# Expert layer with capacity: the last expert's share read straight from its result, sums for two token tiles per addition

## The reference, cut to what matters

```
logits = einsum('GSM,ME->GSE', x, router_w)          # 8 groups of 128 tokens, 8 experts
dispatch, combine = _gating_top2(logits, C)          # C = 32 places per expert and group
expert_inputs = einsum('GSEC,GSM->EGCM', dispatch, x)
hidden = gelu(einsum(expert_inputs, w0)) * einsum(expert_inputs, w1)
expert_outputs = einsum('EGCH,EHM->EGCM', hidden, wo)
out = einsum('EGCM,GSEC->GSM', expert_outputs, combine)
x = x + out
x = x + cross_attention(layernorm(x), ctx, ...)      # the next layer
```

## Time and profile before

| | |
|---|---|
| median of three runs | 1238.1 us |
| the profiled execution's own time | 1238.72 us |
| its span | 1237.0 us (1.7 us lie around it) |
| TensorE busy | 1145.1 us, 93% of the span |
| TensorE weight loads | 732.2 us, 59% |
| VectorE busy | 544.9 us, 44% |
| ScalarE busy | 450.2 us, 36% |
| GpSimd busy | 244.2 us, 20% |
| mean granted TensorE clock | 0.963 |

### The profile page before, as it was taken

One profiled execution on the slowest core, in us unless ns is written; L12 is line 12 of the kernel. 1 busy time (PEld: TensorE's weight loads), 2 busy tenths in 40 slices (PEclk: granted clock), 3 DMA queues, 4 the chain that ended last, 5 costly groups with the idle time before them and its releaser, 6 DMA issues. The chain is left out here.

```text
span 1237.0 us, 19157 instructions
## 1 busy us (share of the span) xinstructions
PE 1145.1 (93%) x7215; PEld 732.2 (59%) x7239; DVE 544.9 (44%) x1553; ACT 450.2 (36%) x591; POOL 244.2 (20%) x366
## 2 busy tenths in 40 slices
PE   6989999999859999999779999999987699999996
PEld 4443333333447888888656333333326699999995
DVE  4657777773362111121157776666406322212111
ACT  4556666666422111111143455555652101110110
POOL 4652222225000000000004000000200233333331
PEclk9999999999959999999989999999998799999998
DMA  8646222001172333345349221120004599999971
GB/s 224 166 150 159 42 40 43 3 1 50 53 273 51 136 136 136 136 147 195 65 180 210 38 39 39 40 40 1 1 1 160 202 372 377 314 321 310 318 231 47
DMA packets 87926, 168.53 MB, mean 136 GB/s; under 512 B 9474, under 2 KB 61396, under 8 KB 85252
## 3 DMA queue, kind: packets, MB, share of 16 engines
q1 hardware_dynamic: 80132, 157.99, 40.5%
q0 software_dynamic: 5152, 6.05, 2.5%
q10 hardware_dynamic: 2560, 3.41, 1.0%
HBM read 147.30 MB, written 20.98 MB: 136 GB/s over the span
## 5 line engine op out<-in xcount | busy, mean ns | idle before, releaser
L1213 ACT ACTIVATE prob<-st_ps 128x1024 f32<-128x1024 f32 x256 | 253.8, 1022 | 186.9 <-PE st_ps L1095 105.0
L219 DVE CUSTOM_DVE_ANT_0 junk<-s_ps,bias_rows,mx 128x512 f32<-128x512 f32 x236 | 167.8, 748 | 64.0 <-PE s_ps L204 63.3
L1087 PE MATMUL st_ps<-q_stack,k_stack 100*128 100x512 bf16 x512 | 183.7, 382 | 7.6 <-ACTq L1188 3.5
L219 DVE CUSTOM_DVE_ANT_0 junk<-s_ps,bias_rows 128x512 f32<-128x512 f32 x232 | 153.3, 689 | 66.0 <-PE s_ps L204 65.5
L204 PE MATMUL s_ps<-k_stack,q_stack 97*128 97x512 bf16 x468 | 174.9, 383 | 7.3 <-ACT q_stack L248 5.4
L1600 PE MATMUL h_ps<-expert_in,w 128*128 (+1 forms) x704 | 155.0, 382 | 2.2 <-PEq L66 2.2
L1600 PEld LDWEIGHTS h_ps<-expert_in,w 128*128 128x128 f32 (+1 forms) x704 | 132.7, 189 | 23.0 <-issue 2.4
L1107 PE MATMUL o_ps<-prob,v_unit 128*32 128x512 f32 x1024 | 139.7, 599 | 1.0 <-ACT prob L1213 1.0
L204 PEld LDWEIGHTS s_ps<-k_stack,q_stack 97*128 97x128 bf16 x468 | 44.8, 98 | 140.2 <-DVE mx L219 83.8
L1946 ACT ACTIVATE silu<-gu_ps 128x512 f32<-128x512 f32 x46 | 27.5, 597 | 227.1 <-PE gu_ps L1887 227.1
L1630 ACT ACTIVATE gelu_out<-h_ps 128x256 f32<-128x256 f32 (+1 forms) x88 | 33.7, 383 | 182.2 <-PE h_ps L1600 182.2
(11 more groups left out here) (283 smaller groups left out, 1185.3 us busy)
## 6 DMA issues: line engine op xcount, KB each, us to landing
wg<-in_gateT SPq DMA_DIRECT2D x23, 1024.0 KB
wu<-in_upT SPq DMA_DIRECT2D x23, 1024.0 KB
wd<-in_downT SPq DMA_DIRECT2D x23, 1024.0 KB
w<-in_w SPq DMA_DIRECT2D x16, 1368.0 KB
w<-in_w SPq DMA_DIRECT2D x8, 1280.0 KB
k_scr<-k_parts SPq DMA_DIRECT2D x48, 128.0 KB, 2.3
k_stack<-k_scr SPq DMA_DIRECT2D x16, 384.0 KB, 4.9
k_stack<-k_scr SPq DMA_DIRECT2D x16, 256.0 KB, 5.6
```

The source lines that it names most:

```text
L219: self.pr.nc.vector.tensor_tensor_reduce(out=self.junk[:, self.bank("job", u, j)], in0=self.ps[:, self.bank("job", u, j)], in1=self.m.bias ...
L1087: pe.matmul(st_ps[:, h], stack(K[b], ROWS, i % 2, h, slice(kt * P, (kt + 1) * P)), stack(Q[b], ROWS, i % 2, h, slice(0, SQ)), start=True, ...
L1213: nc.scalar.activation(prob[:, kt % 2, 2 * hp:2 * hp + 2], st_ps[:, 2 * hp:2 * hp + 2], ACT.Exp).then_inc(exp_done, 1)
```

## The change

For the last expert, the columns of `comb` are turned once more, into the layout in which its result already lies: eight products with 32 output rows each, group 4r + q to partitions 32q of half r, in a bank of the router; VectorE copies them to `comb_last`. After the loop TensorE takes for each group the 128 rows of experts 0 to 3, the 96 rows of experts 4 to 6, and, after the copy of the last result, a product over 32 rows with `comb_last` and `expert_out`. Eight PSUM banks hold the eight sums. VectorE adds two groups at once. The store and the read of the last expert are gone. The second attention layer opens with `stay_warm(8)` ahead of the turning products.

```diff
                 if l == 1:
+                    stay_warm(8)
                     ask.tensor(pe)
                     stay_warm(12)
...
+                    for g in range(NT):
+                        r, at = divmod(g, 4)
+                        mm = pe.matmul(rps[CAP * at:CAP * at + CAP, 0, r * P:(r + 1) * P], comb[:, g, E0 - 1], pr.ident[:],
+                                       start=True, stop=True)
+                    mm.then_inc(last_ready, 1)
...
-                    dve.wait_ge(ct_done, NT // 2)
+                    dve.wait_ge(last_ready, 1)
+                    v.tensor_copy(comb_last[:], rps[:, 0, 0:2 * P].rearrange("p (r n) -> p r n", r=2)).then_inc(ct_done, 1)
+                    dve.wait_ge(ct_done, NT // 2 + 1)
...
+        sums = [h_ps[:, 0:2, 0:D], h_ps[:, 2:4, 0:D], y_ps[:, :, 0:D], e_ps[:, :, 0:D]]
...
                 for e in range(E0 - 1):
                     results_in(e)
-                results_out(E0 - 1)
-                sp.wait_ge(e_out[1], 16)
-                results_in(E0 - 1)
...
-                pe.wait_ge(ec_in, 16 * E0)
-                for g in range(NT):
-                    if g >= 2:
-                        pe.wait_ge(y_done, g - 1)
-                    for h in range(2):
-                        mm = pe.matmul(y_ps[:, g % 2, 0:D], combT[:, h, g * P:(g + 1) * P], ec[h][:, g],
-                                       start=(h == 0), stop=(h == 1))
-                    mm.then_inc(y_ready, 1)
+                pe.wait_ge(ec_in, 16 * (E0 - 1))
+                for r in range(2):
+                    for g in range(4 * r, 4 * r + 4):
+                        if g == 6:
+                            pe.wait_ge(e_copied, E0 + 2)
+                        pe.matmul(sums[g // 2][:, g % 2], combT[:, 0, g * P:(g + 1) * P], ec[0][:, g], start=True, stop=False)
+                        pe.matmul(sums[g // 2][:, g % 2], combT[0:3 * CAP, 1, g * P:(g + 1) * P], ec[1][0:3 * CAP, g], start=False, stop=False)
+                    pe.wait_ge(e_copied, E0 + 2)
+                    for g in range(4 * r, 4 * r + 4):
+                        own = slice(CAP * (g % 4), CAP * (g % 4) + CAP)
+                        mm = pe.matmul(sums[g // 2][:, g % 2], comb_last[own, r],
+                                       eout[own, E0 - 1, r], start=False, stop=True)
+                        if g % 2:
+                            mm.then_inc(y_ready, 1)
...
-                for g in range(NT):
-                    dve.wait_ge(y_ready, g + 1)
-                    nc.vector.tensor_tensor(pr.x[:, g], pr.x[:, g], y_ps[:, g % 2, 0:D], ALU.add).then_inc(y_done, 1)
-
-                    dve.wait_ge(y_done, g + 1)
-                    nc.vector.bn_stats(pr.stats[:, g], pr.x[:, g])
+                for j in range(NT // 2):
+                    two = pr.x[:, 2 * j:2 * j + 2]
+                    dve.wait_ge(y_ready, j + 1)
+                    nc.vector.tensor_tensor(two, two, sums[j], ALU.add).then_inc(y_done, 1)
+                    dve.wait_ge(y_done, j + 1)
+                    for g in (2 * j, 2 * j + 1):
+                        nc.vector.bn_stats(pr.stats[:, g], pr.x[:, g])
```

More of the change, by code:

```diff
@@ L1380, in moe_capacity @@
         combT = pr.sb(c, "comb_T", [P, 2, TOK], F32)
+        comb_last = pr.sb(c, "comb_last", [P, 2, P], F32)
         w_in = [pr.sem(f"w_in{s}") for s in range(2)]
@@ L1403, in moe_capacity @@
             dps = pr.banks(c1, "disp_ps", 2)
+            last_ready = pr.sem("last_ready")
             r_in, l_ready, x_sub, x_exp = pr.sem("r_in"), pr.sem("l_ready"), pr.sem("x_sub"), pr.sem("x_exp")
@@ L1555, in moe_capacity @@
         y_ps = pr.banks(c, "moe_y_ps", 2)
+        sums = [h_ps[:, 0:2, 0:D], h_ps[:, 2:4, 0:D], y_ps[:, :, 0:D], e_ps[:, :, 0:D]]
         h_ready, gelu_done, hid_done, e_ready = (pr.sem(x) for x in ("h_ready", "gelu_done", "hid_done", "e_ready"))
         e_copied, ec_in, y_ready, y_done = (pr.sem(x) for x in ("e_copied", "ec_in", "my_ready", "my_done"))
-        e_out = [pr.sem("e_out_first"), pr.sem("e_out_last")]
+        e_out = pr.sem("e_out")
         with nc.Block() as block:
@@ L1566, in results_out @@
                     sp.dma_start(t["e_scr"][e].rearrange("(r p) m -> p r m", p=P),
-                                 eout[:, e]).then_inc(e_out[e // (E0 - 1)], 16)
+                                 eout[:, e]).then_inc(e_out, 16)
                 def results_in(e):
@@ L1581, in _ @@
                     results_out(e)
-                sp.wait_ge(e_out[0], 16 * (E0 - 1))
+                sp.wait_ge(e_out, 16 * (E0 - 1))
                 for e in range(E0 - 1):
                     results_in(e)
-                results_out(E0 - 1)
-                sp.wait_ge(e_out[1], 16)
-                results_in(E0 - 1)
             @block.tensor
```

## The result

Over 20 runs of each, the kernel before has a median of 1239.91 us (1237.43 to 1243.84) and the change 1232.64 us (1230.09 to 1238.71). The ratio is 0.9949, 95% interval 0.9937 to 0.9962: 0.5% faster, 4.7 to 7.8 us. The forecast was 1232.8 us, with 1230.2 to 1236.6 as its range.

The account below looks back on a forecast made before the run. The bound was the last expert's way through memory, a 6.20 us TensorE wait and slow clock after it, then the second attention's opening chain. Gains 4.5 - 0.5 + 1.3 = 5.3 us gave 1232.8 us, range 1230.2 to 1236.6.

Parts of the forecast that it names:

- The combination: After the last expert: without the wait for memory and the slow clock, the last statistics end 4.5 us sooner.
- a set of four: In the combination: four products over 32 rows, largely working at once, take 0.8 us, between bounds of 0.49 and 1.73.
- VectorE's bare tail: End of the combination: VectorE's last two pairs are not hidden under TensorE's work, 1.5 us each, 3.0 for both.
- The switch of shape: In the combination: changing between product shapes costs at most 0.12 us each, 0.5 for four, covered by the 0.8.
- The routing stage: Ahead of the expert loop: eight added products and a copy cost 0.5 us, at least 0.46, not hidden by anything.
- The opening: Start of the second attention: eight unread products let turning and queries run sooner and faster, +1.3 us, between -2.5 and +2.0.
- queries sooner by 1.0: At the second attention's opening: turning at 2.4 GHz lets the queries start at 634.6 and not 635.62, 1.0 us gained.
- the queries' own clock: At the second attention's opening: the queries' first 1.9 us, at 1.2 GHz before, shrink by 1.0 us.
- the opening stays slow: Rival, chance 0.14: the clock falls at the second attention's opening, the eight products end late, -2.5 us there; 1236.6 us.
- The sum: Whole kernel: combination 4.5, routing stage -0.5 and opening +1.3 give 5.3 us gained.
- Code: Rival, chance 0.05: TensorE waits some 3.6 us for its instructions behind the loop, again at the opening; 1240.0 us.
- The extra gain at the expert loop: Rival, chance 0.11: the clock holds at the expert loop's start, some 1.7 us more gained; 1231.1 us.

Follow-up runs that it names:

- interleaved: The changed kernel with each 32-row product right behind its own tile's wide products, so four never stand together; 1237.44 us, ratio to before 0.9974.
- route_kept: The changed kernel with the last expert's result sent through memory again, the rest of the change staying, `comb_last` unused; 1241.33 us, ratio to before 1.0006.
- change_again: The changed kernel run once more, unaltered, to see what differs between executions; 1233.02 us.
- no_warm: The changed kernel without the eight unread products at the opening of the second attention; 1233.43 us, ratio to before 0.9943.
- filled: The changed kernel with six more unread products on TensorE behind the last 32-row products, while VectorE adds; 1238.53 us, ratio to before 0.9979.
- only_warm: The kernel before with only the eight unread products at the second attention's opening added; 1236.89 us, ratio to before 0.9968.
- small_once: The changed kernel with all eight 32-row products in one set behind the first four tiles, the last four closed pair by pair; 1233.14 us, ratio to before 0.9946.
- filled_quarter: The changed kernel with six more unread products behind the combination and only a quarter of the context read at the opening; 1234.93 us, ratio to before 0.9949.
- small_quarter: The changed kernel with one set of eight 32-row products and only a quarter of the context read at the opening; 1227.99 us, ratio to before 0.9888.

## Why the prediction was right, step by step

- **The combination**, forecast 4.5 us, measured 4.63 (16.09 to 11.46). Its terms: wide products 3.45 a round, measured 3.47; a set of four 0.8, measured 0.74; VectorE's bare tail 3.0, measured 2.84; the loop's exit 0.2, measured none; the 0.6 from the second round's last wide product to VectorE's start 0.84. The errors of up to 0.24 cancel. interleaved shows that the four work at once, route_kept that the removed way through memory is the whole gain at this place. The fall of the clock that the prediction puts 2.6 us after the loop's last product was 2.7: its rows have the end at 610.86, not 610.95; nothing hangs on it.
- **The switch of shape** was taken as at most 0.12 us. TensorE's weight loads show 0.33 of idling at each, and 0.83 us for one 32-row product alone is its 0.43 and 0.20 for each of two switches. The sum stayed because the 0.8 for a set had room: with two such switches, the 0.84 of a set leaves some 0.43 for its products (an estimate), where the prediction's nearest row gave 0.49. The Trainium skill ("TensorEngine Tiling (Array Packing)", Key Properties) says that a change of mode drains TensorE and that its tiles work independently; by both rules, the trace agrees, with 0.33 us of idling and 0.01 us between the starts at 619.18 and 619.19.
- **The routing stage**, forecast -0.5, measured -0.34. I had set 0.46 as the least, one copy and a link; the copy started 0.09 us before the one ahead of it ended (379.67 against 379.76), as the two before it do, of 0.69 each and 1.29 together.
- **The opening**, forecast +1.3, measured +0.65 (23.05 to 22.40 from the last statistics to the score; in change_again +0.20). Of its parts: queries sooner by 1.0, measured 0.05; the queries' own clock 1.0, measured 0.93; the opening's reads, left open, took 0.63; and 0.31 came from the barrier to the norm, which I had not counted. The step that failed is the first: the eight products were to be done when `y_tok` comes. The clock fell, they took 5.38 us and not 3.45, and the turning products waited behind them, one of the signs that the prediction names as wrong. That is the mechanism of its rival "the opening stays slow" (0.14), but without its price of 2.5 us, which needed all eight at 1.2 GHz; the clock rose on the way. Nor are the 0.93 shown to be the eight products' work: no_warm has the same norm to store without them (11.44), its clock back 0.7 us behind the start of the queries, where before it is 1.9. Why it came back sooner there is open.
- **What decides the fall** was argued from the idling. In filled, only_warm, route_kept and small_once the clock holds after 1.01 to 2.45 us of it; in interleaved it falls after 2.43, in the change after 3.80. So a shorter idling is not enough, and what else decides is not shown.
- **The sum**: 5.3 forecast, 4.94 measured in the trace at the places of the change.
- **Code**: the first product started at 611.31 without a gap, and at the opening nothing waited either. **The extra gain at the expert loop** did not come: the clock fell there again (0.69 of 382 to 383). Stretches that run at either clock from one execution to the next do exist, but in the second expert layer and at the end of the second attention.

So the mechanism was right in the combination and in the routing stage, where nearly all of the gain lies. The opening was mis-sized, and half of its mechanism did not happen. That the median came out to 0.2 us is luck: the three runs of before that the forecast starts from gave 1238.1 us, 1.8 less than the 20 do (1239.91), and the gain between the medians is 7.3 us, 2.0 more than the forecast 5.3; the two errors cancel. The changed places give 4.9 of the 7.3. A share of the rest may be how often an execution draws the slow opening of the second expert layer. only_warm's total points the same way: 0.3 us at the score, yet a ratio of 0.9968, and its profile has the fast value, 29.4. Whether a shift of the work by a few us makes the fast draw likelier for a kernel, or whether these sets of runs fell so by chance, stays open; so does filled's median, 3 to 4 us above what its places give. The runs time whole kernels, and only one execution of each has a profile. The prediction passed a gain at the score on in full; the column score to norm (292.8 to 295.4) shows that up to 2.6 us of it can be lost behind it.

The list of TensorE's program of before stands for eight pairs of products in all: seven like the one that is shown follow it, not six.

## What to carry to other kernels

Where a result must change partitions before the next product, look whether the product itself can take it in pieces where it lies, and put the short pieces of different partitions together: four cost what one costs. The gain of the way saved is the wait plus the work that ran at 1.2 GHz after it. Before speeding up what feeds a store, look at what the same DMA engines are doing then: here a store issued up to 1.9 us sooner brought the read-back at most 0.6 us sooner until 1 to 1.5 MB of reads were moved behind the store. And read one execution's profile with care: stretches that the change does not touch moved by 1 to 4 us between two executions of the same kernel.

## What the runs showed of the hardware that was not expected

- One product over 32 rows of float32 between wide ones costs 0.83 us, and a set of four on different rows 0.84 (0.74 from 614.78 to 615.52, and 0.10 on the next wide product), where a wide product costs 0.43. The weight loads idle 0.33 us at each switch of shape.
- The clock held after 1.01, 2.16, 2.43 (route_kept) and 2.45 us without a product, and fell after 2.43 (interleaved) and 3.80 us, within the first 1.1 us of the new work. The Trainium skill ("TensorE: Matmul & The Clock Gate", Part 1) says that where the clock changes varies between runs of one kernel; by that rule, change and change_again agree, 1.97 against 3.42 us for the same instructions.
- A small store that is issued behind 4 MB of reads is done about when they are: its read-back comes 17.5 to 18.6 us after the layer's opening in ten profiles, 1.3 to 2.3 us behind the reads' last packet, and 16.5 with 1.5 MB less ahead of it (filled_quarter, small_quarter). The Trainium skill ("DMA: Bandwidth & Descriptors", Queues, rings and completion order) says that a transfer's signal is written only after all earlier writes of the same DMA engine, whichever queue they are from; by that rule, the read-back can't come before the opening's reads have landed, and the trace agrees, with read-backs within 1.1 us of each other for stores 1.9 us apart.
